# Attention products and depthwise taps on array quadrants, a new stage order, and matmuls of a zeroed tile in early waits

## What is computed

```python
x = x + conv_block(layernorm_over_axis_1(x))       # first half
t = tokens(x)                                      # (4, 1024, 64)
t = t + ffn(layernorm(t))                          # second half
# conv_block:
x_dct = DCT over both spatial axes of x            # 64 x 64, 16 channels
q, k = l2norm(x_tri @ Wq), l2norm(x_tri @ Wk)      # per 8 x 8 window, 4 heads of 16
v = x_tri @ Wv
attn = softmax(einsum('bnhdm,bnhem->bnhde', q, k) * rescale)
x_low = (attn applied to v) @ proj_w + proj_b
h1 = gelu(conv1x1(x_dct, c1a)); h1 = gelu(depthwise3x3(h1, c1b))
x_conv = h1 + x_dct
x_high = gelu(conv1x1(x_conv, c2)) + x_conv
out = inverse DCT of (coef * x_low + (1 - coef) * x_high + x_dct)
# ffn: router, top 2 of 8 experts, each 64 -> 256 -> 64 with an exact gelu
```

## Time and profile before

| | us |
|---|---|
| median of 3 runs (249.52 to 251.16) | 249.86 |
| the profiled execution | 248.42 |
| its span, first to last instruction | 246.4 |
| TensorE matmuls busy | 215.9 (88%) |
| VectorE busy | 153.3 (62%) |
| ScalarE busy | 128.6 (52%) |
| GpSimd busy | 47.0 (19%) |

### The profile page before, as it was taken

One profiled execution on the slowest core, in us unless ns is written; L12 is line 12 of the kernel. 1 busy time (PEld: TensorE's weight loads), 2 busy tenths in 40 slices (PEclk: granted clock), 3 DMA queues, 4 the chain that ended last, 5 costly groups with the idle time before them and its releaser, 6 DMA issues.

```text
span 246.4 us, 3673 instructions
## 1 busy us (share of the span) xinstructions
PE 215.9 (88%) x1462; PEld 125.6 (51%) x1462; DVE 153.3 (62%) x266; ACT 128.6 (52%) x206; POOL 47.0 (19%) x44
## 2 busy tenths in 40 slices
PE   2588779999999965979299999999999999999993
PEld 2476569845755742969242244444444444444430
DVE  0696799997996998396996134444433334444445
ACT  2159731004508263155459676666667777666650
POOL 4670087003833058003210000000000000000000
PEclk9989999999999999999758999999999999999999
DMA  6992000000000000000000674326070714226001
GB/s 213 238 225 40 3 1 3 0 0 0 3 0 1 0 0 0 3 0 0 3 1 13 184 167 100 73 61 154 0 170 3 169 47 124 48 73 144 0 0 43
DMA packets 6592, 14.21 MB, mean 58 GB/s; under 512 B 2736, under 2 KB 4144, under 8 KB 5680
## 3 DMA queue, kind: packets, MB, share of 16 engines
q1 hardware_dynamic: 6576, 13.99, 23.9%
HBM read 12.81 MB, written 1.18 MB: 57 GB/s over the span
## 4 chain that ended last, share of the span: by engine, by line
PE 67%; DVE 18%; ACT 8%; DMA 2%; issue 2%; POOL 1%; SPq 0%; POOLq 0%; DVEq 0%
PE psum L626 23%; PE psum L642 22%; PE psum L484 6%; DVE place L916 4%; PE psum L456 3%; DVE place L994 3%; PE psum L466 3%; DMA sm<-in_small 2%; PE psum L554 2%; ACT place L740 2%; PE psum L563 1%; DVE place L993 1%; DVE st L903 1%; POOL place L837 1%; DVE st L887 1%
## 5 line engine op out<-in xcount | busy, mean ns | idle before, releaser
L626 PE MATMUL psum<-tok,w1s 128*64 128x512 f16 x512 | 61.9, 389 | 0.8 <-ACT w1f L789 0.4
L1088 DVE SCALAR_TENSOR_TENSOR term<-psum,sm,wide 128x512 f32<-128x512 f32 x32 | 24.0, 751 | 61.2 <-PE psum L642 60.5
L789 ACT ACTIVATE hid<-psum,b1p 128x512 f32<-128x512 f32 x64 | 38.6, 701 | 18.7 <-PE psum L626 18.6
L626 PEld LDWEIGHTS psum<-tok,w1s 128*64 128x64 f16 x512 | 28.8, 111 | 36.4 <-issue 8.9
L642 PE MATMUL psum<-hid,w 128*64 128x512 f32 x128 | 28.9, 593 | 0.0
L789 ACT ACTIVATE w1f<-psum,b1p 128x512 f32<-128x512 f32 x32 | 19.5, 688 | 15.2 <-PE psum L626 15.0
L1093 DVE TENSOR_TENSOR x<-x,term 128x512 f32<-128x512 f32 x32 | 22.2, 692 | 1.1
L789 ACT ACTIVATE w1g<-psum,b1p 128x512 f32<-128x512 f32 x32 | 19.6, 714 | 0.3
L642 PEld LDWEIGHTS psum<-hid,w 128*64 128x64 f32 x128 | 9.1, 137 | 15.0 <-issue 9.7
L916 DVE SCALAR_TENSOR_TENSOR place<-h_pad,sm,place 128x512 f32<-128x512 f32 x16 | 15.4, 965 | 0.6
L484 PE MATMUL psum<-h_pad,tap_bd 128*128 128x512 f32 x36 | 15.8, 592 | 0.0
(11 more groups left out here) (141 smaller groups left out, 322.9 us busy)
## 6 DMA issues: line engine op xcount, KB each, us to landing
wide<-gate_store SPq DMA_DIRECT2D x14, 512.0 KB, 6.3
xs<-in_x SPq DMA_DIRECT2D x2, 512.0 KB, 6.0
w1f<-in_W SPq DMA_DIRECT2D x2, 512.0 KB, 11.3
block_out<-x SPq DMA_DIRECT2D x4, 256.0 KB, 6.2
wide<-gate_store SPq DMA_DIRECT2D x2, 384.0 KB, 5.1
hid<-in_W1T SPq DMA_DIRECT2D x1, 512.0 KB, 12.5
w<-in_W SPq DMA_DIRECT2D x1, 512.0 KB, 13.7
c<-const SPq DMA_DIRECT2D x1, 483.5 KB, 4.3
```

Source lines behind the costliest of these rows:

```text
L626: mm = pe.matmul(h_bank(n)[side * H:(side + 1) * H, :], w1s[:, part, e, k * P + side * H:k * P + (side + 1) * H], tok[:, pair, half, b, :] ...
L789: act.activation(hid_of[u % 4][:, t, :], h_bank(n), ACT.Gelu, bias=b1p[:, e * KT + k:e * KT + k + 1]).then_inc(gelu_ready, 1)
L1088: dve.scalar_tensor_tensor(term[:, u % 2, :], y_bank(u), b2t[:, e:e + 1], gate_b[part][:, e % (E // 2), :], ALU.add, ALU.mult).then_inc(te ...
```

## The change

The matmuls of the entry convolution, of the Gram matrices, of their products with the weights, of the norms, the logits, the taps, the projection, `times_wv` and `low` are cut into pieces of 64 rows by 64 columns. For half of the data the row half r is written to the column half 1 - r (`crossed`), so that all four quadrants of the array get work: within a group the image or the set of windows with index `swapped` 0 uses the two quadrants on the diagonal, the other the two off it. The weights of these stages are 64 columns wide, built by GpSimd with two new constant masks (`half_mask`, `half_ident`, 64 columns each, 128 more in the constant transfer that stands ahead of the small weights and of pair 1's input). The taps of both images run on TensorE in one stage `taps`; `first_taps` on VectorE and `gelu_second` are gone. The masks of VectorE cover 64 instead of 128 columns per window. `norms` now writes both banks of its slot, and `taps` waits until VectorE has read them (`norms_read`). A tile `still` of zeros (fp16, 512 columns, set by GpSimd first of all) feeds matmuls into a bank that is free: eight before each `dct_over_h`, six before `windows(0)` and six before `conv_in(0)`. The table of turns is new; the full table is in the diff.

```diff
 TURN = {
-    "weights_of_first": (1, 1), "dct_over_h": (1, 2), "square_columns": (1, 2), "dct_over_w": (3, 5),
-    "windows": (4, 7), "conv_in": (6, 9), "keep_dw": (3, 5), "keep_xd": (4, 7), "gelu_in": (6, 8),
-    "norm_columns": (1, 2), "places": (8, 10), "keep_xt": (9, 10), "join": (2, 4), "high": (3, 5),
-    "gram_matrices": (11, 12), "gram_times_w": (13, 14), "first_taps": (4, 8), "norms": (15, 20), "mask_gram": (5, 6),
-    "second_taps": (16, 21), "logits": (17, 23), "products": (7, 10), "keep_tk": (11, 14), "inverse_norms": (9, 14),
-    "scale_logits": (11, 15), "norms_of_k": (18, 26), "softmax_in": (12, 17), "gelu_second": (12, 19),
-    "softmax_out": (13, 18), "gelu_depthwise": (13, 16), "gelu_out": (15, 22), "conv_out": (19, 27),
-    "project": (22, 29), "exponent": (17, 21), "heads": (24, 30), "times_wv": (25, 31), "keep_y": (18, 23),
-    "low": (28, 35), "mask_mix": (16, 20), "keep_yt": (20, 24), "to_frequencies": (32, 37),
-    "inverse_over_kh": (33, 38), "keep_back": (25, 28), "keep_half": (26, 29), "square_tokens": (27, 31),
-    "mix_branches": (19, 22), "inverse_over_kw": (34, 39), "high_part": (30, 33), "tokens": (36, 40),
-    "residual": (21, 24), "norm_tokens": (23, 25), "keep_tokens": (32, 34), "features": (41, 43), "low_part": (6, 7),
-    "router": (42, 44), "route": (26, 28), "gates_to_rows": (91, 101), "shares": (27, 29), "biases": (3, 3),
-    "tanh_gap": (35, 92), "keep_gates": (91, 101),
+    "weights_of_first": (1, 1), "dct_over_h": (1, 2), "square_columns": (1, 2), "dct_over_w": (3, 6),
+    "windows": (4, 8), "conv_in": (5, 10), "keep_dw": (3, 6), "keep_xd": (4, 8), "gelu_in": (5, 9),
+    "norm_columns": (1, 2), "places": (7, 12), "keep_xt": (7, 10), "join": (2, 4), "high": (3, 5),
+    "gram_matrices": (9, 13), "gram_times_w": (11, 17), "norms": (14, 18), "mask_gram": (3, 7), "taps": (16, 22),
+    "logits": (15, 19), "products": (4, 8), "keep_tk": (11, 13), "inverse_norms": (5, 9), "scale_logits": (6, 11),
+    "norms_of_k": (20, 23), "softmax_in": (10, 13), "softmax_out": (12, 14), "gelu_depthwise": (12, 16),
+    "gelu_out": (14, 20), "conv_out": (21, 26), "project": (24, 28), "exponent": (15, 18), "heads": (25, 30),
+    "times_wv": (27, 31), "keep_y": (17, 21), "low": (29, 33), "mask_mix": (15, 17), "keep_yt": (19, 22),
+    "to_frequencies": (32, 37), "inverse_over_kh": (34, 38), "keep_back": (23, 26), "keep_half": (24, 27),
+    "square_tokens": (25, 29), "mix_branches": (16, 18), "inverse_over_kw": (35, 39), "high_part": (28, 31),
+    "tokens": (36, 40), "residual": (19, 21), "norm_tokens": (20, 22), "keep_tokens": (30, 32), "features": (41, 43),
+    "low_part": (6, 7), "router": (42, 44), "route": (24, 25), "gates_to_rows": (91, 101), "shares": (26, 27),
+    "biases": (23, 23), "tanh_gap": (33, 91), "keep_gates": (101, 102),
 }
...
+            def hold_clock(count, where):
+                for _ in range(count):
+                    pe.matmul(where, still[:, 0:P], still[:, 0:where.shape[1]], start=True, stop=True)
...
             def dct_over_h(p):
+                if p == 0:
+                    pe.wait_ge(still_zero, 1)
+                hold_clock(8, bank(slot(1, 1), 0))
                 pe.wait_ge(x_in[p], 16)
...
             def gram_matrices(p):
                 pe.wait_ge(halo_ready, p + 1)
+                pe.wait_ge(xt_ready, 2 * (p + 1))
+                for q in range(K):
+                    for half in range(2):
+                        for odd in range(2):
+                            v = xt[p][rows_of(odd), q * P + half * H:q * P + (half + 1) * H]
+                            mm = pe.matmul(bank(slot(p, 1), odd)[rows_of(half), q * H:(q + 1) * H], v, v, start=True, stop=True)
+                mm.then_inc(gram_done, 1)
...
             def norms(p):
...
                 for d in range(DH):
-                    mm = pe.matmul(slot(p, 0)[:, 0:2 * G * HEADS], const("pick")[:, DH - 1 - d:DH - 1 - d + P], columns[:, d, :, :],
-                                   start=d == 0, stop=d == DH - 1)
+                    for swapped in range(2):
+                        for half in range(2):
+                            first = DH - 1 - d + half * H
+                            mm = pe.matmul(bank(slot(p, 0), swapped)[rows_of(crossed(half, swapped)), 0:side],
+                                           const("pick")[rows_of(half), first:first + H],
+                                           columns[rows_of(half), d, swapped], start=d == 0, stop=d == DH - 1)
...
-            def second_taps(p):
-
-                pe.wait_ge(tk_ready, 2 * p + 1)
+            def taps(p):
+                pe.wait_ge(norms_read, p + 1)
                 pe.wait_ge(bd_ready, 1)
                 for tap in range(9):
-                    mm = pe.matmul(bank(slot(p, 0), 1), tap_bd[:, tap, :], shifted(p, 1, tap), start=tap == 0, stop=tap == 8)
-                mm.then_inc(second_taps_done, 1)
+                    for b in range(B2):
+                        for half in range(2):
+                            mm = pe.matmul(bank(slot(p, 0), b)[rows_of(crossed(half, b)), :], tap_bd[rows_of(half), tap, :],
+                                           shifted(p, b, tap)[rows_of(half)], start=tap == 0, stop=tap == 8)
+                        if tap == 8:
+                            mm.then_inc(taps_done, 1)
...
             def low(p):
...
+                    for half in range(2):
+                        mm = pe.matmul(slot(p, 1)[rows_of(half), g * H:(g + 1) * H], mix[p][rows_of(half), mix_index(g), :],
+                                       xd[p][rows_of(half), g * H:(g + 1) * H], start=True, stop=True)
...
             def mask_gram(p):
-                for j in range(2):
-                    dve.wait_ge(gram_done, 2 * p + j + 1)
-                    dve.tensor_tensor(gram[p][:, j * K:(j + 1) * K, :], split(slot(p, j), P), mask.unsqueeze(1).broadcast_to([P, K, P]),
-                                      ALU.mult).then_inc(gram_ready, 1)
+                dve.wait_ge(gram_done, p + 1)
+                for odd in range(2):
+                    dve.tensor_tensor(gram[p][:, odd * K:(odd + 1) * K, :], split(bank(slot(p, 1), odd), H),
+                                      half_mask.unsqueeze(1).broadcast_to([P, K, H]), ALU.mult).then_inc(gram_ready, 1)
```

More of the change, by code:

```diff
@@ L114, in constants @@
     out[:, CONST["shifted"]] = block
+    out[:, CONST["half_mask"]] = np.tile(np.kron(np.eye(H // C), np.ones((C, C))), (2, 1))
+    out[:, CONST["half_ident"]] = np.tile(np.eye(H), (2, 1))
     out[:, CONST["diagonal"]] = np.tile(np.eye(DH), (P // DH, 1))
@@ L178, in split, with crossed, rows_of, mix_index @@
             return v.rearrange("p (g h) -> p g h", h=n)
[L180 to L182 removed]
+        def crossed(half, swapped):
+            return 1 - half if swapped else half
+        def rows_of(half):
+            return slice(half * H, (half + 1) * H)
+        def mix_index(g):
+            depth, column, odd = g // K, g % K // 2, g % 2
+            return column % 2 * K + depth * 4 + 2 * odd + column // 2
         c32 = sb("c32", [P, CONST_N])
@@ L244, in metaformer @@
         attn = tk
-        gram = [wide[0][:, p, :].rearrange("p (g n) -> p g n", n=P) for p in range(PAIRS)]
+        gram = [wide[0][:, p, 0:N].rearrange("p (g n) -> p g n", n=H) for p in range(PAIRS)]
         spread_k = [wide[0][:, p, 0:N] for p in range(PAIRS)]
@@ L249, in metaformer @@
         prod = [wide[1][:, p, :].rearrange("p (g n) -> p g n", n=P) for p in range(PAIRS)]
-        mix = [wide[1][:, p, :].rearrange("p (g n) -> p g n", n=P) for p in range(PAIRS)]
+        mix = [wide[1][:, p, 0:N].rearrange("p (g n) -> p g n", n=H) for p in range(PAIRS)]
         h_early = [bank(slot(0, 1), 0), bank(slot(0, 1), 1)]
@@ L537, in low @@
                         pe.wait_ge(mix_ready, 2 * p + g // K + 1)
-                    mm = pe.matmul(slot(p, 0)[:, g * H:(g + 1) * H], mix[p][:, parity(g), :], xd[p][:, g * H:(g + 1) * H], start=True, stop=True)
+                    for half in range(2):
+                        mm = pe.matmul(slot(p, 1)[rows_of(half), g * H:(g + 1) * H], mix[p][rows_of(half), mix_index(g), :],
+                                       xd[p][rows_of(half), g * H:(g + 1) * H], start=True, stop=True)
                     if g % K == K - 1:
@@ L653, in experts @@
                         up(u)
-            stages = (dct_over_h, dct_over_w, windows, conv_in, places, gram_matrices, gram_times_w, norms, logits, second_taps,
+            stages = (dct_over_h, dct_over_w, windows, conv_in, places, gram_matrices, gram_times_w, norms, logits, taps,
                       norms_of_k, conv_out, project, heads, times_wv, low, to_frequencies, inverse_over_kh,
@@ L981, in mask_mix @@
             def mask_mix(p):
+                dve.wait_ge(mix_done, p + 1)
+                blocks = lambda v: v.rearrange("p (o s q n) -> p s o q n", o=2, s=2, n=H)
+                half_masks = half_mask.unsqueeze(1).unsqueeze(1).broadcast_to([P, 2, 4, H])
```

(5 more changed lines are left out.)

179 lines of the change are left out of this document (96 added, 83 removed).

## The result

The changed kernel takes 239.44 us (median of 4 runs, 238.60 to 240.08) against 249.69 of the kernel before, measured beside it: a ratio of 0.958, 95% interval 0.953 to 0.963. The profiled execution took 239.22 us, span 237.1. The forecast was 241.0 us.

The account below looks back on a forecast made before the run. A relay of TensorE and VectorE was taken to set D, the second layer's start. Terms -13.5, +2.4 and +1.9 give -9.2 us; 0.4 given back makes -8.8, so 241.0 us from a 249.86 median, range 236 to 251.

Parts of the forecast that it names:

- D: Start of the first second-layer matmul group on TensorE: 138.96 us before, forecast 127.9.
- the two waits behind it: TensorE waits from late gates: 2.4 us before gates_to_rows(0), and 1.9 us lost at down(3).
- the walk: Step-by-step timing of each engine's new order, a stage starting when engine and data are free: -9.2 us in sum.
- the gates leaving: First gate rows, stored after the moved keep_gates(0): 0.65 us after D, not 4.9 before it.
- What a quadrant costs: Short TensorE instructions on four quadrants: 107 ns at 512 columns, 28 at 128, 27 at 64.
- The bank rule: Skill's rule that different row tiles cannot access one PSUM bank at once; its rival, two quadrants at a time: 264 us, 0.08.
- the router's 25 ns: Start-to-start time of the router's 16 eight-column matmuls, taken as the issue pace for short instructions.
- Rival E: Short instructions take 13 to 20 ns each, 2 to 4 us less, 237 to 239 us; chance 0.11.
- its own signs of being wrong: Tap groups of 15 us, norm groups of 5 or 7, half clock in middle stages, or gates in time.
- The zeroed matmuls: Matmuls filling waits before dct_over_h, windows(0) and conv_in(0): -0.5 to +0.6 us, taken as 0.
- nothing follows from a faster first DCT: At pair 0's first DCT: VectorE's chain waits for the small weights until 7.97 us, so full clock there gains nothing.
- the 6.1 us that the walk gives Gram(0): Gram(0) starts at 25.6 us instead of 31.72, from shorter GpSimd and VectorE work, reordered stages and conv_in(0).

Follow-up runs that it names:

- e3: The changed kernel with route, shares, tanh_gap and keep_gates in the order of the kernel before, biases left late: 235.84 us.
- e5: The changed kernel with the 72 tap matmuls of each pair issued image by image instead of interleaved: 249.29 us.
- e8: The changed kernel with biases early, the gate stages in their old order and 22 more zeroed matmuls in two later waits: 232.10 us.
- e1: The changed kernel without its 28 zeroed matmuls: 240.79 us.
- e4: The changed kernel with every stage at its turn in the kernel before, and without zeroed matmuls: 249.92 us.
- e9: e4 with one turn changed, VectorE's inverse_norms(1) ahead of softmax_out(0) instead of behind it: 248.29 us.
- e6: The changed kernel with image 0's taps back on VectorE, ahead of the masks, image 1's left on TensorE: 257.94 us.

## Why the prediction was right, and where it was not

**D and the two waits behind it.** The time was right within 1.6 us, and the walk held to its last steps: D 127.68 for 127.9, the gates leaving at D + 0.72 for 0.65, and the third group of the second layer (w1g) at D + 10.53 instead of D + 8.65 before, so 1.88 us lost for 1.9. e3 gives just this back: span less D is 107.4 again. The wait ahead of gates_to_rows(0) was 0.99 us for 2.4, since TensorE got there at 120.82 (121.81 - 0.99), 1.3 later than the walk had it: there was half clock in most of the way from 108 us, and features(1) was held 0.99 us by a GpSimd cast of 3.27 us that ran beside `biases`. The start of the stage, 121.81, was forecast as 121.95.

**What a quadrant costs.** Right for long instructions: 107 ns at 512 columns, 27 at 128 (Gram times w, 64 in 1.95 us, of which the last record is 0.27). The bank rule that the prediction set against the change shows nowhere: halves on the diagonal share a bank and all four quadrants work at once (72 in 7.94 us; e5 shows what two at a time would be). Wrong for 64 columns on four quadrants: not 27 ns but (2.10 - 0.27)/127 = 14, where 0.27 is one record. The step that failed was to take the router's 25 ns as a pace of the issue; those matmuls were all on one tile. So in this term Rival E came true (13 to 20 ns, chance 0.11), and 1.5 us were ahead at the end of taps(1) (64.7 for 66.2).

**Where these 1.5 us went.** To the clock. At to_frequencies(0) they were still there: it began at 84.06, and the forecast 94.1 for to_frequencies(1), less the 8.70 us that lie between the two at full clock (e8), gives 85.4. But TensorE had waited 2.08 us, half clock followed, and 0.9 + 0.7 us went in two stages; to_frequencies(1) began at 94.33, forecast 94.1. e8 shows the cause: with that wait filled, both stages run at full clock. The stop in norms(0) took another 1.4 us of the gain, and so norms(0) ended at the 38.2 that had been forecast for slower instructions. The walk had neither, and a half clock in the middle stages was one of its own signs of being wrong. That the total came so near is in part luck: the short instructions were quicker than forecast, and a stop and a half clock that were not in it took that back.

**The zeroed matmuls** are the term that was mis-sized: put at 0 (-0.5 to +0.6), they are worth 3.6 us at Gram(0), 1.6 at D in this kernel and 2.5 in e8. Two steps failed. One said that nothing follows from a faster first DCT, since VectorE waits for the small weights: in e1 VectorE waited 1.02 us longer, for the copy of that DCT, and 1.1 us of the 3.6 come from there. The other kept the stages' lengths as they had been. In the kernel before, pair 1's DCT stood right before dct_over_w(0), which ran at full clock:

```profile
14.76 2.02 PE L407 MATMUL psum<-c,place 128*128 128x128 f32 x16
```

In e1 pair 1's input is there at 9.05, not at 11.26; TensorE then waits 2.19 us ahead of dct_over_w(0), and the clock falls (3.65 us). e4 and then e9, the same kernel up to there and both without zeroed matmuls, show that this hangs on when the input comes:

```profile
10.47 3.78 PE L420 MATMUL psum<-c,xs 128*128 128x128 f32 x16 [1.93 <-DMA xs<-in_x]
14.04 2.04 PE L430 MATMUL psum<-c,place 128*128 128x128 f32 x16
```

```profile
8.95 2.96 PE L420 MATMUL psum<-c,xs 128*128 128x128 f32 x16 [0.23 <-DMA xs<-in_x]
13.97 3.46 PE L430 MATMUL psum<-c,place 128*128 128x128 f32 x16 [2.06 <-DVE place L961]
```

Why it comes early or late wasn't looked into, so the 3.6 us are the worth in one execution, not the mean. In that execution most of the 6.1 us that the walk gives Gram(0) were theirs: e1 keeps 2.3 of it. At Gram(0) the walk was right because it had credited to the chain and the order what the clock gave.

**The order.** The walk never priced the quadrants without it. e4 does: nothing is gained by shorter instructions when VectorE reads the norms 7 us after they are there. The cut matmuls gain nothing without the new order, and e5 and e6 show that taking away the overlap of the quadrants in the taps or the move of the taps costs 10 and 18 us. The new order with the matmuls left uncut wasn't run, so what the order brings by itself isn't known.

**A version beyond both.** e8, with its gates on time and two more waits filled, takes 232.1 us, 3% less than the change (0.929 against 0.958 of before).

## What to carry to other kernels

Packing an engine's instructions pays only as far as the engine that it relays with is ready, so re-time the whole relay with the new lengths and price the packing in the old order too. Each wait that an improvement opens on TensorE, like those of 2 us here, can bring a half clock behind it: check the granted clock after every new wait, and fill those waits with work that hinders nobody. Interleave the instructions of different quadrants one by one; image by image, the same work took 1.8 times as long here (14.0 for 7.94 us).

## What the runs showed of the hardware

Starts on different quadrants come every 14 ns, though 16 matmuls on one tile came every 25. The Trainium skill (TensorE: Matmul & The Clock Gate, Wait — 56ns, not 53.3ns?) gives about 25 ns as the least time from start to start; the norms (128 in 2.10 us) say that this does not bind across quadrants.

TensorE stood 0.28 to 1.40 us behind its 474th matmul record in eleven runs, whatever stage that fell in, and the stop ended 2.2 to 2.8 us after a 16 KB packet of instructions. In e6, after a wait of 8.40 us just ahead, it did not stop there. The Trainium skill (Runtime: NRT & Kernel Launch, Instruction fetch mechanics) describes blocks of 16 KiB, 256 instructions, fetched while the current ones run, and calls the cost mostly hidden. That the short matmuls outran their instructions, and that this packet is the one TensorE stood for, fits the times and wasn't shown; if it is so, the cost is not hidden here.

Whether the clock falls in a wait of about 2 us changes with the moment: after 2.08 us at 82 us it fell in the changed kernel, after 2.06 us at 85 us it did not in e1, and after 2.06 us at 12 us it did in e9. So one execution shows a cost of the clock of which another kernel with the same stages is free.
